# Decoder layer on one core: the transpose of the softmax reciprocals placed behind the second pair of scores of the next unit

## The chip, the cores and the metric

The kernel runs on one core of a Trainium2 chip. The time is the device time of one execution in microseconds (us). The kernel before took 1795.61 us, the median of 3 runs (1793.44 to 1797.07).

## What is computed

A decoder layer on x, 8 batches of 512 tokens with width 512, in float32: a dilated self-attention within segments of 128 tokens, a cross-attention over a context, and a feed-forward block whose activations and weights are quantised in blocks of 32. Each of the three is added to x. The edit touches the cross-attention alone (16 heads of 32, 512 queries, the first 512 rows of the context, causal):

```
qp = q @ Wq.T
kv = latent_kv @ Wkv_expand.T
k, v = jnp.split(kv, 2, axis=-1)
scores = jnp.einsum('bhqd,bhkd->bhqk', qh, kh) * inv_sqrt_d
scores = jnp.where(causal, scores, jnp.finfo(scores.dtype).min)
attn = jax.nn.softmax(scores, axis=-1)
out = jnp.einsum('bhqk,bhkd->bhqd', attn, vh)
return out.transpose(0, 2, 1, 3).reshape(b, sq, H) @ Wout.T
```

## The kernel before

First come the weights (0 to about 203 us). Then each batch has two stages: the cross-attention (about 93 us) and a stage with the feed-forward block of this batch and the self-attention and layer norms of the next (about 108 us). Every engine has a fixed program, written out by hand, and they wait for one another by semaphores.

**Units.** The cross-attention works on units (oc, qt): oc is a group of four heads (4 a batch), qt a tile of 128 queries (T = 4). By the causal mask a unit has (qt + 1) x 128 keys, so qt 0 is the smallest unit and qt 3 the largest. The work of three units overlaps. In the iteration of unit u:
- TensorE makes the scores of u + 1 in two pairs of heads (score2, L1099 to L1115), turns the reciprocals of u - 1 (turn_recip, L1132 to L1136) and multiplies the probabilities of u - 1 with v (values2, L1138 to L1155), and transposes the four heads' probabilities of u (turn_p2, L1117 to L1130). For the next oc it projects the queries (project_q, at qt 2, twelve matmuls of 512 columns) and the keys (project_k, at qt 0). In the last oc, qt 1 and 2, it makes part of the first output tile (output) in their place.
- VectorE finds the rows' maxima of the scores (maxima, L770), copies the transposed heads 0 and 2 into pt2 (take_probs, L783), and makes the reciprocals of the row sums and spreads them to 32 columns a head (recips, L789 and L792, tile recip_x). Once an oc it multiplies the values with the transposed reciprocals (take_out, L798, tile xn, which out_n shares).
- ScalarE makes the exponentials with their sums (exps, L969), copies the transposed heads 1 and 3 into pt2 (take_probs, L993) and the transposed reciprocals into recip_t (take_recip, L983), and casts keys and queries of the next oc (high_k, high_q).

**PSUM.** psum_plan (L57) lays down in which order the results take their turns in each piece of PSUM. A result may be written when the one ahead of it in that list has been read (until_free); who needs the reader's work waits by until_freed. A and B hold the first and second pair of scores (two banks each). C0 and C1 are one bank each: C0 takes heads 0 and 2 of the transposed probabilities, C1 takes heads 1 and 3 and, behind them, the transposed reciprocals. T and O, one bank each, take keys, queries and values (outT) of even and odd oc in turn: the keys of oc + 1 go into the bank from which take_out has read the values of oc - 1.

**Waits around the change.** turn_recip waits for its turn in C1 and for recip_x. values2 waits for the copies of heads 2 and 3 in pt2, and at qt 0 for its bank; it doesn't wait for the reciprocals. take_out waits for the last values product of its oc and for the copy of its last reciprocals in recip_t.

Of the kernel before, what the change touches and what calls it, by code (L numbers as in the profile page):

```python
# [56 lines left out]
def psum_plan(B, T, OC):  # L57

    plan = {s: [] for s in ("T", "O", "A", "B", "C0", "C1")}
    turn = [0]  # L60

    def self_attention(b, i):
        for label in self_attention_step(b, i, T):
            plan[("T", "C1")[turn[0] % 2]].append(label)
            turn[0] += 1

    P1_STEPS = 4 * T + 5
    for i in range(P1_STEPS):
        self_attention(0, i)

    def head(b, i):
        for t in HEAD_TILES[i]:
            plan[("C1", "A", "B", "C1")[t]].append(("xT2", b * T + t))

    for i in range(4 * T, P1_STEPS):
        head(0, i)
    for b in range(B):
        for oc in range(b * OC, (b + 1) * OC):

            plan["TO"[oc % 2]].append(("k", oc))  # L80
            plan["TO"[oc % 2]] += [("q", oc), ("outT", oc)]
            for qt in range(T):
                for pr in range(2):
                    plan["AB"[pr]].append(("scores2", oc, qt, pr))
                for hh in range(4):
                    plan[f"C{hh % 2}"].append(("probsT2", oc, qt, hh))
                plan["C1"].append(("recipT", oc, qt))
        for t in range(T):
            plan["TABO"[t]].append(("y", b * T + t))
        for i in range(P1_STEPS):  # L90
            if i < 4 * T:
                if i % 4 == 0:
                    plan["C0"].append(("xqT", b * T + i // 4))
                plan["AB"[i % 2]].append(("gateup", 4 * T * b + i))
            if INTER_LAG <= i < 4 * T + INTER_LAG:
                plan["C0"].append(("interT", 4 * T * b + i - INTER_LAG))
            if b + 1 < B:
                self_attention(b + 1, i)
                if i >= 4 * T:
                    head(b + 1, i)  # L100
        for t in range(T):
            plan["O"].append(("down", b * T + t))
    return plan


def decoder_layer(nc, x, ctx_t, wq_t, wkv_t, wo_t, w_gate, w_up, w_down, out):
# [3 lines left out]
    T = N // P  # L110
    C = D // P
    OC = C
# [13 lines left out]
    with es:  # L126
# [537 lines left out]
        with nc.Block() as block:  # L664
# [77 lines left out]
            def _(dve):  # L742
# [137 lines left out]
                for b in range(B):  # L880

                    first, end = b * UNITS, (b + 1) * UNITS
                    for pr in range(2):
                        maxima(first, pr)
                    for u in range(first, end):
                        oc, qt = units[u]
                        more = oc % OC + 1 < OC
                        if u + 1 < end:
                            maxima(u + 1, 0)
                        take_probs(u, 0)  # L890
                        if qt == 0 and oc % OC:
                            take_out(oc - 1)
                        if qt == 1 and more:
                            low_k(oc + 1)
                        if qt == 2 and more:
                            low_q(oc + 1)
                        if u + 1 < end:
                            maxima(u + 1, 1)
                        take_probs(u, 1)
                        recips(u)  # L900
                    take_out((b + 1) * OC - 1)

                    last = b + 1 == B
                    take_y(b * T)
                    moments3(b * T)
                    take_y(b * T + 1)
                    quantise_x(b * T)
                    take_y(b * T + 2)
                    moments3(b * T + 1)
                    round_x(b * T)  # L910
                    if not last:
                        attend_vector(dve, link, b + 1, 0)
                    take_y(b * T + 3)
                    if not last:
                        attend_vector(dve, link, b + 1, 1)
                    for i in range(P1_STEPS):
                        if i < CHUNKS:
                            gated(b * CHUNKS + i)
                        if 1 <= i <= CHUNKS:
                            round_inter(b * CHUNKS + i - 1)  # L920
                        if i in STATS_AT:
                            moments3(b * T + STATS_AT[i])
                        if i % 4 == 3 and i > 4:
                            take_down(b * T + i // 4 - 1)
                        if i >= 2 and not last:
                            attend_vector(dve, link, b + 1, i)
                            head(b + 1, i)
                        if i % 4 == 0 and i // 4 + 1 < T:
                            quantise_x(b * T + i // 4 + 1)
                        if i % 4 == 1 and i // 4 + 1 < T:  # L930
                            round_x(b * T + i // 4 + 1)

            @block.scalar
            def _(act):
# [94 lines left out]
                for b in range(B):  # L1029

                    first, end = b * UNITS, (b + 1) * UNITS
                    for pr in range(2):
                        exps(first, pr)
                    for u in range(first, end):
                        oc, qt = units[u]
                        if u > first:
                            take_recip(u - 1)
                        more = oc % OC + 1 < OC
                        if u + 1 < end:
                            exps(u + 1, 0)  # L1040
                        if qt == 1 and more:
                            high_k(oc + 1)
                        if qt == 2 and more:
                            high_q(oc + 1)
                        take_probs(u, 0)
                        take_probs(u, 1)
                        if u + 1 < end:
                            exps(u + 1, 1)
# [17 lines left out]
            def _(pe):  # L1066
# [160 lines left out]
                for b in range(B):  # L1227
# [4 lines left out]
                    for u in range(first, end):  # L1232
                        oc, qt = units[u]
                        more = oc % OC + 1 < OC
                        if u + 1 < end:
                            score2(u + 1, 0)
                        if u > first:
                            turn_recip(u - 1)
                            values2(u - 1)
                        if qt == 2 and more:  # L1240
                            project_q(oc + 1)
                        turn_p2(u, 0)
                        if u + 1 < end:
                            score2(u + 1, 1)
                        turn_p2(u, 1)
                        if qt == 0 and more:
                            project_k(oc + 1)
                        if not more and 0 < qt < 3:

                            output(b * T, [0, 1] if qt == 1 else [2])  # L1250
# [49 lines left out]
```

How the kernel before makes its waits and increments, by code:

```python
        def until_free(pe, label):  # L211
            s, k = slot_of[label]
            if k:
                pe.wait_ge(freed[s], k)
# [4 lines left out]
        def until_filled(eng, label):  # L219
            s, k = slot_of[label]
            eng.wait_ge(filled[s], k + 1)
# [1 line left out]
        def until_freed(eng, label):  # L223
            s, k = slot_of[label]
            eng.wait_ge(freed[s], k + 1)
# [60 lines left out]
            @block.sync  # L286
            def _(sp):
                for j in range(RAW):
                    load_weights(sp, j)
                sp.dma_start(wq_raw[:], wq_t.rearrange("(c p) n -> p c n", p=P)).then_inc(wq_loaded, 16)
                sp.dma_start(wkv_raw[:], wkv_t).then_inc(wkv_loaded, 16)
                sp.dma_start(wo_sb[:], wo_t.rearrange("(c p) n -> p c n", p=P)).then_inc(wo_loaded, 16)
                for j in range(STEPS - RAW):
                    sp.wait_ge(wy_ready, j + 1)
                    load_weights(sp, j + RAW)
                sp.wait_ge(wo_loaded, 16)
# [5 lines left out]
                def link(ins):  # L303
                    n[0] += 1
                    ins.then_inc(pool_chain, 1)
                    pool.wait_ge(pool_chain, n[0])
# [16 lines left out]
                def scaled_rows(j):  # L323
                    pool.wait_ge(wr_ready, j + 1)
                    if j >= 2:
                        pool.wait_ge(wclip_ready, j - 1)
                    pool.tensor_tensor(by_block(w_y[:, j % 2]), by_block(w_raw[:, j % RAW]), spread(w_r[:, j]),
                                       ALU.mult).then_inc(wy_ready, 1)
```

## Time and profile before

| | before |
|---|---|
| three runs, median (lowest to highest) | 1795.61 us (1793.44 to 1797.07) |
| the profiled execution | 1798.01 us |
| span of its trace | 1796.2 us |
| mean granted TensorE clock | 0.908 of full speed |
| TensorE matmuls (PE) | 1435.2 us, 80% of the span |
| TensorE weight loads (PEld) | 874.5 us, 49% |
| VectorE (DVE) | 1178.7 us, 66% |
| ScalarE (ACT) | 861.2 us, 48% |
| GpSimd (POOL) | 547.4 us, 30% |
| shares of the chain that ended last | PE 43%, DVE 29%, ACT 9%, issue 9%, POOL 2% |

The table is of one profiled execution; its span runs from the first to the last instruction of the trace, and 1.8 us lie around it. Busy shares are averages over stages with different limits. In the timelines, PE is a matmul or transpose and PEld the weight load ahead of it; consecutive instructions of one line stand in one row (x6: six of them), and a number in brackets is the time for which the engine had been idle before it, with what it waited for.

### The profile page before, as it was taken

To read this page: it belongs to the slowest core of one execution; us is meant where nothing else is said; L and a number is where in the kernel's file an instruction comes from. 1 tells how busy PE (TensorE), PEld (TensorE's weight loads), DVE (VectorE), ACT (ScalarE), POOL (GpSimd) and SP (SyncE) were. 2 spreads that over 40 slices of the span, in tenths; PEclk is the share of its full clock that TensorE was granted. 3 is DMA by queue.
4 is the path that set the end of the run, shared out by engine and by line. 5 is a ranking of instruction groups with operands and counts; after the bars stand their busy time and mean duration, and the time that the engine had idled before them with its cause. 6 is when DMAs were issued, how large, how long until landed. Compare 5 with 4: busy or idle time off the path is not lost.

```text
span 1796.2 us, 31869 instructions
## 1 busy us (share of the span) xinstructions
PE 1435.2 (80%) x11616; PEld 874.5 (49%) x11616; DVE 1178.7 (66%) x2539; ACT 861.2 (48%) x2098; POOL 547.4 (30%) x494
## 2 busy tenths in 40 slices
PE   1224899789988899889988899879988899789987
PEld 0113565446634565446644565446644565446633
DVE  8993455865578555865577556865578555865576
ACT  2442454455635554455635554455635554455522
POOL 5871000640046101640046101640046100640045
PEclk9999899998999899898998799897999899998998
DMA  5311000010000001010000000010000000000001
GB/s 181 112 46 36 1 1 25 7 25 1 2 24 13 18 1 24 7 24 1 2 24 13 18 2 24 7 24 1 2 24 13 18 1 25 7 19 1 2 1 24
DMA packets 25287, 36.10 MB, mean 20 GB/s; under 512 B 2480, under 2 KB 10672, under 8 KB 25136
## 3 DMA queue, kind: packets, MB, share of 16 engines
q1 hardware_dynamic: 25136, 34.09, 7.1%
q8 instruction: 95, 1.56, 0.4%
q14 instruction: 56, 0.46, 0.1%
HBM read 25.69 MB, written 8.39 MB: 19 GB/s over the span
## 4 chain that ended last, share of the span: by engine, by line
PE 43%; DVE 29%; ACT 9%; issue 9%; POOL 2%; DMA 0%; SPq 0%; ACTq 0%; DVEq 0%; POOLq 0%
PE psum L526 9%; PE psum L1110 7%; PE psum L1127 7%; PE psum L1148 5%; DVE top L820 5%; PE psum L1164 4%; DVE inter L846 3%; DVE nmx L770 3%; PE psum L1187 3%; PE psum L1209 2%; PE psum L1113 2%; DVE q L816 2%; ACT silu L1007 2%; DVE pt L783 2%; PE psum L1136 2%
## 5 line engine op out<-in xcount | busy, mean ns | idle before, releaser
L503 POOL TENSOR_TENSOR rstd<-var_eps,minus_half 128x1 f32<-128x1 f32 x96 | 59.8, 623 | 894.9 <-DVE var_eps L497 894.9
L969 ACT ACTIVATE p<-psum,nmx 128x384 f32<-128x384 f32 (+3 forms) x512 | 265.8, 526 | 68.4 <-DVE nmx L770 64.0
L770 DVE TENSOR_REDUCE nmx<-psum 128x2 f32<-128x256 f32 (+3 forms) x256 | 210.7, 823 | 114.6 <-PE psum L1113 114.6
L783 DVE COPY pt<-psum 128x128 f32<-128x128 f32 (+3 forms) x256 | 124.6, 487 | 193.9 <-PE psum L1127 193.5
L1127 PE MATMUL psum<-ident,p 128*128 128x128 f32 x1280 | 206.4, 289 | 21.1 <-ACT pt L993 18.1
L1110 PE MATMUL psum<-k_hl,q_hl 32*128 32x128 f32 (+3 forms) x1536 | 204.3, 373 | 16.4 <-DVE q_hl L757 11.7
L691 POOL TENSOR_TENSOR inter<-inter,rscale 128x512 f32<-128x512 f32 x128 | 141.3, 1104 | 209.8 <-DVE rscale L854 209.2
L1209 PE MATMUL psum<-wd_sb,iq_t 128*128 128x512 bf16 x512 | 147.6, 415 | 37.8 <-DVE x_res L863 28.1
L993 ACT COPY pt<-psum 128x128 f32<-128x128 f32 (+3 forms) x256 | 109.3, 427 | 141.6 <-PE psum L1127 140.2
L1127 PEld LDWEIGHTS psum<-ident,p 128*128 128x128 f32 x1280 | 143.8, 146 | 56.0 <-ACT pt L993 26.6
L1187 PE MATMUL psum<-wg_sb,xq_t 128*128 128x512 bf16 x512 | 148.9, 418 | 26.2 <-ACT xq_t L1000 21.7
L1110 PEld LDWEIGHTS psum<-k_hl,q_hl 32*128 32x128 f32 x1536 | 124.5, 199 | 77.2 <-issue 53.7
L1187 PE MATMUL psum<-wu_sb,xq_t 128*128 128x512 bf16 x512 | 147.6, 415 | 0.0
L846 DVE TENSOR_TENSOR inter<-psum,silu 128x512 f32<-128x512 f32 x128 | 86.6, 677 | 85.8 <-ACT silu L1007 85.2
L691 POOL TENSOR_TENSOR iq<-q,scale 128x512 bf16<-128x512 fp8e4 x128 | 142.8, 1115 | 0.4 <-DVE q L816 0.4
L1007 ACT ACTIVATE silu<-psum 128x512 f32<-128x512 f32 x128 | 76.0, 593 | 126.3 <-PE psum L1187 126.0
L1164 PE MATMUL psum<-wo_sb,xn 128*128 128x512 f32 x256 | 124.8, 639 | 6.5 <-DVE xn L798 6.5
L526 PE MATMUL psum<-x_t,wq_hl 128*128 128x512 f32 (+1 forms) x480 | 126.1, 421 | 1.4 <-DVE k_hl L764 1.1
L1015 ACT COPY iq_t<-psum 128x512 bf16<-128x512 bf16 x128 | 74.5, 582 | 87.3 <-PE psum L1198 87.3
L427 PE MATMUL psum<-ident_b,w_q 128*128 128x128 bf16 x192 | 26.3, 310 | 112.3 <-POOL w_q L334 108.3
L526 PEld LDWEIGHTS psum<-x_t,wq_hl 128*128 128x128 f32 x480 | 96.3, 232 | 29.0 <-issue 10.0
L1148 PE MATMUL psum<-pt,v_sb 128*32 128x128 f32 x2560 | 105.8, 296 | 0.0
(104 smaller groups left out, 2397.5 us busy)
## 6 DMA issues: line engine op xcount, KB each, us to landing
x_in<-in_x_dram SPq DMA_DIRECT2D x32, 256.0 KB, 4.1
out_dram<-x_res SPq DMA_DIRECT2D x64, 128.0 KB, 2.4
w_raw<-in_w_gate_dram SPq DMA_DIRECT2D x16, 256.0 KB, 2.8
w_raw<-in_w_up_dram SPq DMA_DIRECT2D x16, 256.0 KB, 3.2
w_raw<-in_w_down_dram SPq DMA_DIRECT2D x16, 256.0 KB, 3.8
ctx_in<-in_ctx_t_dram SPq DMA_DIRECT2D x8, 256.0 KB, 2.9
wq_raw<-in_wq_t_dram SPq DMA_DIRECT2D x1, 1024.0 KB, 8.0
wo_sb<-in_wo_t_dram SPq DMA_DIRECT2D x1, 1024.0 KB, 10.2
```

What stands on the lines that cost most here:

```text
L526: last = pe.matmul(dst, w, x, start=(n == 0), stop=(stop and n == len(terms) - 1))
L691: pool.tensor_tensor(dst.rearrange("p (n k) -> p n k", k=BLOCK), src.rearrange("p (n k) -> p n k", k=BLOCK), scales.unsqueeze(2).to_broadc ...
L770: dve.tensor_reduce(nmx2[:, u % UNITS, 2 * pr:2 * pr + 2], where(("scores2", oc, qt, pr))[:, :, 0:(qt + 1) * P], AX_X, ALU.max, negate=Tru ...
L783: free(dve.tensor_copy(pt2[:, hh, 0:m], where(label)[:, 0, 0:m]), label)
L846: free(dve.tensor_tensor(inter[:, r, :], where(label)[:, 1, :], silu[:, i % 2, :], ALU.mult), label)
L969: ins = act.activation(p2[:, (4 * u + hh) % P2_RING, 0:m], where(label)[:, hh % 2, 0:m], ACT.Exp, bias=nmx2[:, u % UNITS, hh:hh + 1], accu ...
L1110: pe.matmul(where(label)[:, j, 0:m], q_hl[rows, oc % 2, i, qt * P:(qt + 1) * P], k_hl[rows, oc % 2, k, 0:m], start=(n == 0), stop=False)
L1127: last = pe.transpose(where(label)[:, 0, kt * P:(kt + 1) * P], p2[:, (4 * u + hh) % P2_RING, kt * P:(kt + 1) * P], ident[:])
L1148: last = pe.matmul(where(("outT", oc))[rows, 0, qt * P:(qt + 1) * P], v_sb[:, kt, h * HD:(h + 1) * HD], pt2[:, hh, kt * P:(kt + 1) * P], s ...
L1164: last = pe.matmul(where(label)[:, 0, :], out_n[:, oc, t % T * P:(t % T + 1) * P], wo_sb[:, oc, :], start=(oc == 0), stop=(oc == OC - 1))
L1187: last = pe.matmul(where(label)[:, j, :], xq_t[:, t % 2, c * P:(c + 1) * P], w[:, c, m * CH:(m + 1) * CH], start=(c == 0), stop=(c == C - 1))
L1209: last = pe.matmul(where(label)[:, 0, :], iq_t[:, i % RING, j * P:(j + 1) * P], wd_sb[:, 4 * m + j, :], start=(m == 0 and j == 0), stop=(m ...
```

## The change

In TensorE's order turn_recip(u - 1) moves from its place ahead of values2(u - 1) to a place behind the second score2 of the iteration and ahead of the transposes of heads 2 and 3 of u. The turns in C1 follow: head 1 of u, the reciprocals of u - 1, head 3 of u. Only the very last reciprocals of a batch keep a turn behind head 3 of their own unit. On ScalarE take_recip(u - 1) moves from the start of the iteration to between the copies of heads 1 and 3. On VectorE take_out(oc - 1) moves behind the maxima of the second pair of scores, ahead of the copy of head 2. No instruction is added or taken away, and no wait changes its condition but for the turns in C1.

```diff
--- before.py
+++ after.py
@@ -83,8 +83,11 @@
                 for hh in range(4):
+                    if hh == 2 and (qt or oc % OC):
+                        plan["C1"].append(("recipT", *((oc, qt - 1) if qt else (oc - 1, T - 1))))
                     plan[f"C{hh % 2}"].append(("probsT2", oc, qt, hh))
-                plan["C1"].append(("recipT", oc, qt))
+                if qt == T - 1 and oc % OC == OC - 1:
+                    plan["C1"].append(("recipT", oc, qt))
@@ -888,14 +891,14 @@
                         take_probs(u, 0)
-                        if qt == 0 and oc % OC:
-                            take_out(oc - 1)
                         if qt == 1 and more:
                             low_k(oc + 1)
                         if qt == 2 and more:
                             low_q(oc + 1)
                         if u + 1 < end:
                             maxima(u + 1, 1)
+                        if qt == 0 and oc % OC:
+                            take_out(oc - 1)
                         take_probs(u, 1)
                         recips(u)
@@ -1033,8 +1036,6 @@
                         oc, qt = units[u]
-                        if u > first:
-                            take_recip(u - 1)
                         more = oc % OC + 1 < OC
@@ -1043,6 +1044,8 @@
                         take_probs(u, 0)
+                        if u > first:
+                            take_recip(u - 1)
                         take_probs(u, 1)
@@ -1235,13 +1238,14 @@
                         if u + 1 < end:
                             score2(u + 1, 0)
                         if u > first:
-                            turn_recip(u - 1)
                             values2(u - 1)
                         if qt == 2 and more:
                             project_q(oc + 1)
                         turn_p2(u, 0)
                         if u + 1 < end:
                             score2(u + 1, 1)
+                        if u > first:
+                            turn_recip(u - 1)
                         turn_p2(u, 1)
```

## Rows read from the trace of the kernel before

**Rows 1.** The page of the profile, its first line.
```profile
span 1796.2 us, 31869 instructions
```

**Rows 2.** Busy time by stage: us, busy by engine, granted clock, DMA share, GB/s.
```profile
404.00:497.00 93.00, 84.70 (x787) 57.21 (x787) 50.12 (x104) 54.06 (x179) 0.00 (x0) 0.89 0.01 1
...
699.00:807.00 108.00, 89.72 (x643) 48.35 (x644) 80.81 (x197) 47.89 (x78) 55.79 (x56) 0.91 0.10 23
...
900.00:1008.00 108.00, 91.03 (x625) 48.77 (x625) 80.00 (x196) 46.24 (x72) 55.88 (x56) 0.87 0.09 23
```

**Rows 3.** The waits, whole span: us in total, times, longest us.
```profile
PE psum L1136 <- DVE recip_x L792: 39.4, 64, 0.9
```

**Rows 4.** Timeline, qt 3: start us, us, engine, line, operation [idle, releaser].
```profile
447.60 0.55 DVE L783 COPY pt<-psum 128x384 f32<-128x384 f32 x1
...
448.63 0.30 PE L1136 MATMUL psum<-ident,recip_x 128*128 128x128 f32 x1 [0.86 <-DVE recip_x L792]
...
448.86 0.86 PE L1148 MATMUL psum<-pt,v_sb 128*32 128x128 f32 x24
```

**Rows 5.** Timeline: the same period, rest of qt 3, start of qt 0.
```profile
450.79 0.58 ACT L993 COPY pt<-psum 128x512 f32<-128x512 f32 x1 [0.76 <-PE psum L1127]
...
451.28 1.04 PE L1127 MATMUL psum<-ident,p 128*128 128x128 f32 x8
...
452.36 0.58 ACT L993 COPY pt<-psum 128x512 f32<-128x512 f32 x1 [0.99 <-PE psum L1127]
...
453.34 1.08 PE L1148 MATMUL psum<-pt,v_sb 128*32 128x128 f32 x32
```

**Rows 6.** Timeline: the same period, qt 0, up to the key projection.
```profile
454.92 0.68 DVE L798 TENSOR_TENSOR xn<-psum,recip_t 128x512 f32<-128x512 f32 x1
...
455.39 0.39 PE L1127 MATMUL psum<-ident,p 128*128 128x128 f32 x2
455.59 0.69 DVE L770 TENSOR_REDUCE nmx<-psum 128x2 f32<-128x512 f32 x1
...
455.66 0.96 PE L526 MATMUL psum<-ctx_hl,wkv_hl 128*128 128x512 f32 x3
```

**Rows 7.** Timeline: the same period, qt 1, up to the next values product.
```profile
457.70 0.27 ACT L983 COPY recip_t<-psum 128x128 f32<-128x128 f32 x1 [0.37 <-PE psum L1136]
...
460.62 0.44 PE L1127 MATMUL psum<-ident,p 128*128 128x128 f32 x2 [0.84 <-ACT pt L993]
...
460.99 0.96 PE L1110 MATMUL psum<-k_hl,q_hl 32*128 32x512 f32 x6
...
462.94 0.75 PE L1148 MATMUL psum<-pt,v_sb 128*32 128x128 f32 x16
```

**Rows 8.** Timeline: the last oc of the batch (qt 1, 2 and 3).
```profile
482.31 0.37 ACT L993 COPY pt<-psum 128x256 f32<-128x256 f32 x1
...
483.00 1.88 PE L1164 MATMUL psum<-wo_sb,xn 128*128 128x512 f32 x4
...
489.17 0.55 PE L1127 MATMUL psum<-ident,p 128*128 128x128 f32 x3 [0.21 <-ACT pt L993]
...
489.56 1.02 PE L1164 MATMUL psum<-wo_sb,xn 128*128 128x512 f32 x2
...
491.07 0.86 PE L1148 MATMUL psum<-pt,v_sb 128*32 128x128 f32 x24
...
492.99 0.58 ACT L993 COPY pt<-psum 128x512 f32<-128x512 f32 x1 [1.25 <-PE psum L1127]
...
495.18 0.30 PE L1136 MATMUL psum<-ident,recip_x 128*128 128x128 f32 x1 [0.78 <-DVE recip_x L792]
```

**Rows 9.** Chain that ended last, three query projections: start us, us, what.
```profile
642.03 4.01 PE psum L526 x12
...
843.45 4.01 PE psum L526 x12
...
1047.56 4.31 PE psum L526 x12
```

## The prediction

> **What bounds the kernel now.** I read the busy times by stage first, then the waits, then the timeline of one period. The profiled execution spans 1796.2 us [rows 1]. Each of the eight batches has an attention stage of about 93 us, in which TensorE's matmuls are busy 84.7 us [rows 2], and a longer second stage that the edit leaves alone. In the attention stage TensorE works through a fixed order, so its own row sets the end: whatever moves an instruction there moves all behind it. Where it idles, the waits say for whom; the largest single wait of this stage is the transpose of the reciprocals (turn_recip, L1136) waiting for VectorE's copy recip_x: 39.4 us in 64 places [rows 3]. The edit aims at that wait. So the question is what else those places wait for, and what the transpose meets where it is put instead. For that one period (four units, 440.6 to 463.6 us) is walked on TensorE's row, and the last one of the batch separately. A gap in another engine's row counts only if TensorE stands at its end.
>
> **Part 1, the old place.** In the iteration of qt 3 TensorE idles 0.86 us, transposes at 448.63 and starts the values product at 448.86 [rows 4]. Without the transpose the product still needs pt2 of head 2, which VectorE copies from 447.60 to 448.15. A copy's end is seen about 0.06 us later (the product with ctx starts at 455.66, after take_out's end at 455.60 [rows 6]). So it starts at 448.20: **-0.66 us**. In the iteration of qt 0 it needs ScalarE's copy of head 3, 452.36 to 452.94 [rows 5]; with 0.06 to 0.23 us of signalling, of which I take 0.15 for the later of two waits, it starts at 453.09, against 453.34: **-0.25**. I take no extra cost for going from the scores straight to the values product: the nearest row has 0.23 us between the transpose and the product [rows 4], so it lies between 0 and 0.2.
>
> **Part 2, the new place.** Now the order in bank C1 is head 1, reciprocals, head 3. Before, one use lay between two copies by ScalarE, and score2 and head 2 (bank C0) covered it; now there are two uses, with only head 2's transposes between the second pair. From the start of the reciprocals' transpose, its 0.30 us [rows 4], 0.04, ScalarE's copy of 0.27 [rows 7] and 0.06 make about 0.63 us until head 3's transposes may start. The transpose itself takes 0.11 us of TensorE's time (eight in 1.04 us, the last of them about 0.27 long [rows 5]), and head 2's take 0.11 for each of qt+1 tiles. Left uncovered: about 0.4, 0.3, 0.2 and 0.1 us for qt 0, 1, 2 and 3.
> - qt 3: head 1's copy ends at 451.37 and head 2's transposes start at 451.28 [rows 5]. The reciprocals, put ahead of them, wait 0.15 for that copy, take 0.11, and head 3 waits 0.08: **+0.35**.
> - qt 0 followed by a project_k (twice a batch, for oc 1 and 2): take_out now also stands behind the second maxima on VectorE. These start at 455.59 and keep it some 0.60 us; take_out is ready no sooner (455.39 + 0.58 for the copy of recip_t), runs 456.20 to 456.88, and project_k, which needs its bank, starts at 456.94 instead of 455.66 [rows 6]: **+1.28**. With no project_k behind it (oc 3): 0.63 instead of 0.11 from head 2's old start to head 3, **+0.52**. What is queued behind the moved take_out on VectorE (head 2's copy, the next reciprocals) ends before the next scores do.
> - qt 1: here TensorE already idles 0.84 us ahead of head 3 for ScalarE's copy of head 1, until 460.62 [rows 7], since that copy stands behind two exponentials, which wait for maxima, and behind high_k. So an earlier values product brings nothing: the reciprocals start at 460.62, drag head 2 behind them, and head 3 comes at 461.25: +0.63. The next scores start at 461.62 instead of 460.99 and last about 1.05 with the causal part; the values product follows at once, at 462.68, against 462.94 [rows 7]. Together **-0.25**.
> - qt 2: transpose 0.11 and head 3's wait of 0.2 are swallowed, since the next values product hangs on VectorE's copy behind the maxima of scores that came earlier: **0** (at most +0.3).
>
> **Part 3, the last oc.** No project_k there, so ScalarE's copy of head 1 hangs on the maxima in each iteration. qt 1: it ends at 482.68, the reciprocals start at 482.73, head 3 at 483.37, the output at 483.67 against 483.00 [rows 8]: +0.66. qt 2: head 3 waited for the same copy at 489.17 [rows 8]; all of that moves by 0.66, and the output comes another 0.63 later than head 3 did: 490.86 against 489.56. It lasts 0.9, and the values product follows it at 491.76 against 491.07: +0.69. qt 3: head 1's copy ends at 493.57 + 0.69, the reciprocals start at 494.31, head 3 at 494.95, its four transposes and its copy end 1.2 later, and the last reciprocals' transpose, which needs C1, starts at 496.23 against 495.18 [rows 8]. In all **+1.05**.
>
> **The sum.** Per batch: three passages from qt 3 to qt 0, 3 x (-0.66 + 0.35 - 0.25) = -1.68; the k waits, 2 x 1.28 + 0.52 = 3.08; three iterations of qt 1, 3 x (-0.25) = -0.75; the last oc +1.05. That is +1.70 us, times 8 = **+13.6 us** on the span of 1796.2. The table's profiled execution took 1798.0 with 1.8 outside its span, 2.4 over the median of the three runs, 1795.6; on that median the forecast is **1809 us**. Nothing is removed: the same 128 transposes and copies run. DMA queues and GpSimd have nothing in this stage that the edit passes. The open costs (0 to 0.2 us for going from scores to values, some 15 times a batch but mostly within a wait; up to 0.3 at qt 2; take_out's reach) give +1.1 to +2.4 per batch, so 1804 to 1815.
>
> **The rivals.**
> - **The clock falls further.** The granted clock of the attention stage is 0.89 of full speed, a mean over stretches at 2.4 and at 1.2 GHz. What a change in it costs shows once: the second stage at 900 to 1008 us was granted 0.87 against 0.91 one batch before [rows 2], and the query projections of that batch start 204.1 us apart instead of 201.4 [rows 9]: 2.7 us. The edit makes the longest stretch with few matmuls (after the scores of qt 0, to project_q) about 1.5 us longer. The same price in each batch: 13.6 + 21.6 = 35, so **1831**. Against it: the moved waits also close gaps elsewhere, and the mean hardly has to fall.
>  The Trainium skill states this rule in "TensorE: Matmul & The Clock Gate", section "A second HAM failure mode: psum-queue depth-cycling": cycling through PSUM banks with short idles between groups of matmuls makes the clock swing between full and half rate. The trace agrees so far that 0.89 is granted in a stage in which TensorE is nearly always busy; by the rule the change would come out at this rival's time.
> - **The clock rises**, by the same price with less dense work in front of it: 13.6 - 21.6, so **1788**.
> - **take_out is in time.** If project_k finds its bank as early as head 3 allows, 2 x (1.28 - 0.52) = 1.5 us a batch fall away and +0.2 is left: **1797**, no change. For it: VectorE idles a good deal here. Against it: maxima of 0.69 us stand right in front of take_out.
> - **The advances stay (the other side).** If the way through C1 is covered, by other work of TensorE between the reciprocals and head 3, only gains are left: 3 x (-0.91) for qt 3 and 0 and 3 x (-0.88) for qt 1, with 15 x 0.11 for the transposes: -3.7 a batch, **1766**. It decides at one point: whether TensorE comes to head 3 later than 0.63 us after the reciprocals. Against it: between them stand at most four transposes of 0.11, and at qt 1 ScalarE's copy of head 1 is late already.
>
> **How the numbers follow.** Forecast 0.60; take_out in time 0.12; clock falls 0.16, half of it not beyond 1823; clock rises 0.07; advances stay 0.05. The range leaves out the two faster cases and the far half of the falling clock, 0.20: 1797 to 1823. About 0.2% is what a measurement of this kernel can tell from no change, here 1792 to 1799. Faster 0.12, same 0.12, slower 0.76.
>
> **What would show it.** Right: the wait of the reciprocals' transpose for recip_x is gone, and in its place it waits for pt L993 about once a period for over 1 us and in the last oc three times; head 3's transposes wait for ScalarE's recip_t in most units; project_k waits for take_out (xn) by about 0.7 us twice a batch; the projections lie 0.4 to 0.5 us further apart. Wrong: head 3 never waits for recip_t, or the values product still starts at the old distance from the scores, or the stage is shorter at the same clock. A mean clock of the stage off 0.89 by more than 0.02 would spoil the size in either direction.

## The result and the profile after

The change takes 1824.34 us (median of 4 runs, 1823.63 to 1824.99) against 1794.53 us before (4 runs): a ratio of 1.0165, 95% interval 1.0147 to 1.0182. It is 30 us slower. The forecast had the sign and less than half of the size: 1809 us, with a range that ended at 1823. One of the four executions of one experiment (take_out back at its old place) took 2559 us and is left out of its figure.

The head of the page after; the columns are busy time, share of the span and number of instructions:

```profile
span 1822.0 us, 31800 instructions
## 1 busy us (share of the span) xinstructions
PE 1447.9 (79%) x11547; PEld 879.9 (48%) x11616; DVE 1180.2 (65%) x2539; ACT 862.9 (47%) x2098; POOL 547.3 (30%) x494
```

The attention stage of one batch before, from its first scores to its last values product (stretch, its length, busy time of each engine, granted clock, DMA share, GB/s), and of one batch after:

```profile
804.70:899.00 94.30, 85.94 (x799) 58.33 (x803) 50.55 (x105) 55.31 (x184) 0.00 (x0) 0.89 0.01 1
```

```profile
1023.80:1121.70 97.90, 89.50 (x803) 58.58 (x803) 50.72 (x105) 55.43 (x184) 0.00 (x0) 0.88 0.01 1
```

The stage is 3.6 us longer; six of the eight batches after have 97.8 to 97.9 us, where six before had 94.3 to 94.5. The other two after take 99.5 and 100.6 us at a granted clock of 0.86 and 0.85, the other two before 95.2 and 95.5 us at 0.87 (each to the end of its last instruction, which adds some 0.25). The eight attention stages together are 30.3 us longer. The stage behind them has 107 us in most batches of both kernels. VectorE and ScalarE are as busy as before. TensorE's matmuls are busy 3.6 us longer, though they are the same matmuls: in part they ran at a lower clock.

The waits after, in total, times and longest us:

```profile
ACT recip_t L986 <- PE psum L1139: 63.1, 128, 0.8
...
PE psum L1139 <- ACT pt L996: 40.9, 48, 1.2
PEld psum L1130 <- ACT recip_t L986: 36.8, 120, 0.5
```

The wait of the reciprocals' transpose for recip_x, 39.4 us before [rows 3], is gone. In its place the same transpose (now L1139) waits 40.9 us for ScalarE's copy of head 1, and the weight loads of head 3's transposes (PEld, L1130) wait for the copy of the reciprocals in 120 places; in 24 of these TensorE's matmuls stand still as well, 6.0 us in all.

The timeline after, one period of TensorE's work, of the same kind as in [rows 4 to 7], from one query projection to the next:

```profile
859.36 3.84 PE L529 MATMUL psum<-x_t,wq_hl 128*128 128x512 f32 x12
...
864.79 0.28 PE L1139 MATMUL psum<-ident,recip_x 128*128 128x128 f32 x1
...
866.74 0.86 PE L1151 MATMUL psum<-pt,v_sb 128*32 128x128 f32 x24
...
869.30 0.33 PE L1139 MATMUL psum<-ident,recip_x 128*128 128x128 f32 x1
...
870.57 0.62 PE L1113 MATMUL psum<-k_hl,q_hl 32*128 32x256 f32 x6
870.68 0.59 ACT L996 COPY pt<-psum 128x512 f32<-128x512 f32 x1 [0.74 <-PE psum L1130]
...
871.41 1.08 PE L1151 MATMUL psum<-pt,v_sb 128*32 128x128 f32 x32
...
873.46 0.28 PE L1139 MATMUL psum<-ident,recip_x 128*128 128x128 f32 x1
...
873.66 0.69 DVE L773 TENSOR_REDUCE nmx<-psum 128x2 f32<-128x512 f32 x1 [0.58 <-PE psum L1116]
...
874.10 0.33 PE L1130 MATMUL psum<-ident,p 128*128 128x128 f32 x1 [0.25 <-ACT recip_t L986]
874.27 0.68 DVE L801 TENSOR_TENSOR xn<-psum,recip_t 128x512 f32<-128x512 f32 x1
...
875.01 0.96 PE L529 MATMUL psum<-ctx_hl,wkv_hl 128*128 128x512 f32 x3 [0.58 <-DVE xn L801]
...
879.53 0.39 ACT L996 COPY pt<-psum 128x256 f32<-128x256 f32 x1
...
879.97 0.33 PE L1139 MATMUL psum<-ident,recip_x 128*128 128x128 f32 x1 [1.19 <-ACT pt L996]
...
881.03 1.18 PE L1113 MATMUL psum<-k_hl,q_hl 32*128 32x512 f32 x6
...
882.47 1.08 PE L1151 MATMUL psum<-pt,v_sb 128*32 128x128 f32 x16
...
883.48 1.88 PE L529 MATMUL psum<-x_t,wq_hl 128*128 128x512 f32 x4
```

The reader is to see three things. The values products start as soon as their copies are there (866.74, 871.41). The key projection stands until take_out is done (875.01). And at qt 1 TensorE idles 1.19 us until ScalarE's copy of head 1 ends; the reciprocals and head 2 start only then. The last rows tell something that the forecast did not have: the scores at 881.03 take 1.18 us where before they took 0.96, and sixteen values matmuls 1.08 where before they took 0.75 [rows 7]. The stretch from these scores to the next projection, before and after, with the granted clock third from the end:

```profile
460.99:463.62 2.63, 2.09 (x27) 1.11 (x26) 2.60 (x6) 1.77 (x6) 0.00 (x0) 0.95 0.01 3
```

```profile
881.03:883.48 2.45, 2.45 (x25) 1.21 (x24) 1.75 (x5) 1.51 (x5) 0.00 (x0) 0.62 0.01 3
```

Before, almost all of it ran at 2.4 GHz; after, some three quarters of it ran at 1.2 GHz.

The period is 24.1 us against 23.05. The chain that ended last has the projections of one batch after:

```profile
1040.05 3.91 PE psum L529 x12
1064.27 3.74 PE psum L529 x12
1088.44 3.63 PE psum L529 x12
```

### The profile page after: what moved, and what is told of

The parts are those of the page before. It is cut to its first block, busy times and chain, and to the rows that moved or that the text cites. A ratio compares the mean times of both kernels' runs of the same rounds, so it can differ in the third digit from the quotient of the medians.

```text
span 1822.0 us, 31800 instructions
## 1 busy us (share of the span) xinstructions
PE 1447.9 (79%) x11547; PEld 879.9 (48%) x11616; DVE 1180.2 (65%) x2539; ACT 862.9 (47%) x2098; POOL 547.3 (30%) x494
## 4 chain that ended last, share of the span: by engine, by line
PE 45%; DVE 25%; ACT 11%; issue 8%; POOL 2%; DMA 0%; ACTq 0%; SPq 0%; DVEq 0%; POOLq 0%
PE psum L529 9%; PE psum L1113 8%; PE psum L1130 7%; PE psum L1151 5%; DVE top L823 4%; DVE nmx L773 3%; PE psum L1167 3%; PE psum L1190 3%; DVE inter L849 3%; PE psum L1116 2%; PE psum L1212 2%; ACT p L972 2%; ACT silu L1010 2%; DVE xn L511 1%; PE psum L1139 1%
## 5 line engine op out<-in xcount | busy, mean ns | idle before, releaser
L1130 PE MATMUL psum<-ident,p 128*128 128x128 f32 x1280 | 224.5, 294 | 10.9 <-ACT recip_t L986 6.0
L1113 PE MATMUL psum<-k_hl,q_hl 32*128 32x128 f32 (+3 forms) x1536 | 211.8, 384 | 15.6 <-DVE q_hl L760 11.7
L1130 PEld LDWEIGHTS psum<-ident,p 128*128 128x128 f32 x1280 | 148.8, 146 | 63.6 <-ACT recip_t L986 36.8
L1190 PE MATMUL psum<-wg_sb,xq_t 128*128 128x512 bf16 x452 | 133.8, 417 | 40.6 <-ACT xq_t L1003 30.0
L1167 PE MATMUL psum<-wo_sb,xn 128*128 128x512 f32 x256 | 114.6, 596 | 6.5 <-DVE xn L801 6.5
L1212 PEld LDWEIGHTS psum<-wd_sb,iq_t 128*128 128x128 bf16 x512 | 51.9, 108 | 127.3 <-issue 54.3
```

The source lines that it names most:

```text
L1113: pe.matmul(where(label)[:, j, 0:m], q_hl[rows, oc % 2, i, qt * P:(qt + 1) * P], k_hl[rows, oc % 2, k, 0:m], start=(n == 0), stop=False)
L1130: last = pe.transpose(where(label)[:, 0, kt * P:(kt + 1) * P], p2[:, (4 * u + hh) % P2_RING, kt * P:(kt + 1) * P], ident[:])
L1167: last = pe.matmul(where(label)[:, 0, :], out_n[:, oc, t % T * P:(t % T + 1) * P], wo_sb[:, oc, :], start=(oc == 0), stop=(oc == OC - 1))
L1190: last = pe.matmul(where(label)[:, j, :], xq_t[:, t % 2, c * P:(c + 1) * P], w[:, c, m * CH:(m + 1) * CH], start=(c == 0), stop=(c == C - 1))
L1212: last = pe.matmul(where(label)[:, 0, :], iq_t[:, i % RING, j * P:(j + 1) * P], wd_sb[:, 4 * m + j, :], start=(m == 0 and j == 0), stop=(m ...
```

## The experiments

Two questions were open: how much of the 30 us is waits and how much clock, and which of the moves costs. The runs were made in four groups, each on one chip and beside runs of the kernel before: 1795.0 us for the first four kernels, 1797.2 for the next four, 1797.2 and 1795.8 for two each. Ratios are to the kernel before.

**The transpose directly behind the values product.** This takes the wait for recip_x away from the values product, and leaves C1, ScalarE and VectorE as before.

```diff
--- before.py
                         if u > first:
-                            turn_recip(u - 1)
                             values2(u - 1)
+                            turn_recip(u - 1)
```

> The kernel before with turn_recip directly behind values2 instead of ahead of it; turns in C1, ScalarE and VectorE as before. Theory (the loss of the change lies in where the transpose was put, not in taking it away from ahead of the values product): the values product no longer waits for recip_x and starts 0.66, 0.25 and 0.5 us earlier at qt 3, 0 and 1; the way through C1 (0.63 us) is covered by head 0's transposes alone, so head 1 waits 0.3 us at qt 0 and 0.15 us at qt 1. The projections come 22.7 us apart instead of 23.05, and the time is 1781 us (-1.7 us a batch). Rival (the values product wins nothing, as the maxima and exponentials set the pace): 1792 to 1796 us, projections 23.0 us apart.

Measured: **1765.3 us**, 0.9825 (0.9798 to 0.9853), 30 us faster than before. The theory holds in direction: the values product does win its time if the transpose goes to a place where the way through C1 is covered. Its size is double the forecast. The stage and two projections of this kernel:

```profile
791.70:882.80 91.10, 85.25 (x803) 56.72 (x803) 50.74 (x105) 55.59 (x184) 0.00 (x0) 0.91 0.01 2
```

```profile
829.20 3.00 PE L526 MATMUL psum<-x_t,wq_hl 128*128 128x512 f32 x12
...
832.04 0.82 PE L1127 MATMUL psum<-ident,p 128*128 128x128 f32 x6
...
850.78 4.13 PE L526 MATMUL psum<-x_t,wq_hl 128*128 128x512 f32 x12
```

The twelve matmuls of a projection take 3.65 us or more in every batch of the kernels before and after. Here the second projection of each batch takes 3.0, at 2.4 GHz throughout; the first still takes 3.6 to 4.3, and the third 3.0 in four batches and 4.1 in the other four. So a part of the gain is clock: the stage is granted 0.91, against 0.89. How much is waits can be read where this kernel and the kernel before with a filled wait (below) have the same clock. One stage of this kernel, then one of that:

```profile
989.54:1079.33 89.79, 83.94 (x803) 55.72 (x803) 50.73 (x105) 55.76 (x184) 0.00 (x0) 0.92 0.01 1
```

```profile
796.64:888.94 92.30, 86.44 (x819) 57.94 (x819) 50.75 (x105) 55.32 (x184) 0.00 (x0) 0.93 0.01 1
```

That is 2.5 us a batch, an estimate of 20 us in all for the waits, where 1.7 a batch was expected; about 10 us came by the clock.

**The transpose between head 2 and head 3.** The change, with less of TensorE's own work behind the transpose.

```diff
--- after.py
                     for hh in (2 * pr, 2 * pr + 1):
+                        if hh == 3 and u % UNITS:
+                            turn_recip(u - 1)
...
-                        if u > first:
-                            turn_recip(u - 1)
                         turn_p2(u, 1)
```

> The change, but with the transpose of the reciprocals between head 2 and head 3 instead of ahead of head 2; turns in C1 as in the change. Theory (the price is the way from the transpose through ScalarE's copy to head 3): nothing of TensorE's own work is left in between, so head 3 waits 0.54 us in every unit instead of 0.1 to 0.4, and the time is 12 us above the change: about 1837 us. Rival (the price is that head 2 is held back with the reciprocals at qt 1, and VectorE's copy behind it): head 2 goes out early again, and the time is 5 to 10 us below the change: 1815 to 1819 us.

Measured: **1845.0 us**, 1.0278 (1.0258 to 1.0298), 21 us slower than the change. So the price is the way through C1 to head 3: TensorE's matmuls now wait for the copy of the reciprocals in 120 places, 42.7 us. Head 2 goes out early again and nothing is won by it on balance; what it alone is worth isn't shown. The size is again larger than the waits that were worked out, and the clock of the stage fell to 0.87.

**Four wide matmuls in the wait of qt 1**, in the change and in the kernel before. They do no useful work; they fill time in which TensorE stands.

```diff
--- after.py
+                def fill(u, count):
+                    oc, qt = units[u]
+                    label = ("probsT2", oc, qt, 2)
+                    until_free(pe, label)
+                    for _ in range(count):
+                        pe.matmul(where(label)[:, 0, :], ident_b[:], wg_sb[:, 0, 0:512], start=True, stop=True)
...
+                        if qt == 1:
+                            fill(u, 4)
                         if u > first:
                             turn_recip(u - 1)
                         turn_p2(u, 1)
```

> The change with four more bf16 matmuls of 512 columns in each iteration of qt 1, into bank C0 (whose turn they take just ahead of head 2) and ahead of the transpose of the reciprocals: at 2.4 GHz they last 0.9 us and lie in the 1.2 us for which TensorE waits there anyway. Their results are overwritten. Theory (what the change lost beyond the forecast 13.6 us, some 16 us, is the lower granted clock, 0.878 in the attention stage against 0.891): the clock of the stage rises above 0.90, the projections come under 23.7 us apart instead of 24.15, and the time is 1805 to 1815 us. Rival (the excess is waits and switching between kinds of matmul): clock about as in the change or the time unmoved, 1822 to 1830 us.

> The kernel before with the same four matmuls at qt 1, ahead of head 2's transposes; TensorE waits 0.84 us there for ScalarE's copy of head 1. Clock theory: the stretches at 1.2 GHz ahead of and in the query projections vanish, the clock of the attention stage rises from 0.89 to above 0.92, and the time is 1780 to 1790 us. Rival (waits alone): 1794 to 1800 us at the same distance of the projections.

Measured: in the change **1789.2 us** (0.9971, 0.9957 to 0.9985), 35 us below the change without them; in the kernel before **1768.5 us** (0.9845, 0.9824 to 0.9866), 27 us faster than before. More work made both kernels faster. In the change the whole gain lies in the attention stages (32.9 us between the two traces); in the kernel before 16 of 28 us do, and 8 lie in the stages behind them and 4 ahead of the first batch. The stages, first in the change and then in the kernel before:

```profile
1005.30:1099.50 94.20, 88.48 (x819) 57.42 (x819) 50.82 (x105) 55.41 (x184) 0.00 (x0) 0.93 0.01 1
```

```profile
994.60:1086.60 92.00, 86.15 (x815) 57.91 (x819) 50.74 (x105) 55.21 (x184) 0.00 (x0) 0.93 0.01 2
```

Both are granted 0.93, and there the change costs 2.2 us a batch (94.2 against 92.0), where at their own clocks it costs 3.6. So about 2.2 us a batch, 18 us in all, are waits, and about 1.4 us, 11 us in all, came by the clock. The forecast for the waits was 1.7. The split is an estimate: it takes the added matmuls to cost both kernels the same. At qt 1 behind a key projection they cost neither anything: from the scores behind that projection to those behind the wait it stays 5.13 us in the change and 4.45 in the kernel before. In the first oc they run at 1.2 GHz and take twice as long, in both.

**The same four, narrow.** A control: about the same time (1.0 us for the four at 2.4 GHz, as for the wide ones), on a sixteenth of the array.

```diff
--- the change with the wait filled
-                        pe.matmul(where(label)[:, 0, :], ident_b[:], wg_sb[:, 0, 0:512], start=True, stop=True)
+                        pe.matmul(where(label)[0:HD, 0, :], ident_b[0:HD, 0:HD], wg_sb[0:HD, 0, 0:512], start=True, stop=True)
```

> The change with four matmuls at the same place and of the same 512 columns as in the run with the filled wait, but on 32 rows and 32 columns of the array instead of 128 by 128, so that they take the same time and fill the same wait with little work for the array. Clock theory (the gain of the filled wait came from the clock, which follows the work done in the array): the clock of the attention stage stays near 0.88 and the time within 4 us of the change, 1820 to 1828 us. Rival (it is enough that TensorE doesn't stand idle, or the four matmuls shift the order of the waits): about 1789 us as with the wide ones, the clock again near 0.93.

Measured: **1821.5 us**, 1.0141 (1.0108 to 1.0174).

```profile
813.70:911.20 97.50, 91.86 (x815) 58.77 (x819) 50.79 (x105) 55.23 (x184) 0.00 (x0) 0.89 0.00 1
```

The stage has 97.5 us and a clock of 0.89, close to the 97.9 and 0.88 without any. The order of the waits is the same in both filled kernels, so the 32 us between them come from what the four matmuls do in the array, by way of the clock. But the narrow ones weren't without effect. The start of a stage and the rest of it, first narrow, then wide:

```profile
813.72:835.20 21.48, 20.96 (x108) 12.53 (x109) 7.83 (x16) 9.65 (x35) 0.00 (x0) 0.52 0.00 1
835.20:911.50 76.30, 71.20 (x712) 46.30 (x711) 42.96 (x89) 45.72 (x149) 0.00 (x0) 1.00 0.01 1
```

```profile
803.55:818.40 14.85, 14.20 (x76) 8.44 (x76) 6.34 (x14) 6.71 (x26) 0.00 (x0) 0.54 0.00 0
818.40:898.10 79.70, 74.41 (x744) 48.86 (x743) 44.48 (x92) 48.76 (x158) 0.00 (x0) 1.00 0.01 2
```

In seven of the eight batches the narrow ones, too, left no stretch at 1.2 GHz behind the start of the stage, where every stage of the change has two; there the second period is 22.57 us in both. They lose at the start: the clock stays at 1.2 GHz until 21.5 us into the stage, with the wide ones until 14.8, and in the change until 18.3.

**take_out back at its old place, and take_out moved alone.** The two halves of one question: what does VectorE's part of the change cost?

```diff
--- after.py (first kernel); before.py with the signs exchanged (second kernel)
                         take_probs(u, 0)
+                        if qt == 0 and oc % OC:
+                            take_out(oc - 1)
...
                             maxima(u + 1, 1)
-                        if qt == 0 and oc % OC:
-                            take_out(oc - 1)
```

> The change with take_out back at its old place on VectorE, ahead of the maxima of the second pair. Theory (project_k waits because the last reciprocals of an oc are transposed and copied so late, not because of VectorE's order): take_out starts 0.15 us earlier and project_k still waits over 0.4 us; the time is within 4 us of the change. Rival (the maxima in front of take_out make the wait): project_k comes 0.8 us earlier twice a batch, -13 us, 1811 us.

> The kernel before with the move of take_out alone, behind the maxima of the second pair. Theory: these start at 455.6 in the period that was read and take_out only behind them, so project_k comes 1.2 us later, twice a batch, and little of it is made good, +2.5 to +3.0 us a batch: 1815 to 1820 us, and project_k waits for xn in 16 places. With a lower clock on top up to 1830. Rival (VectorE has room, the wait is swallowed by the ScalarE copy for which TensorE waits at qt 1): 1795 to 1800 us.

Measured: back at its old place **1825.0 us** (three executions, 1823.6 to 1834.4; ratio 1.0178, 1.0135 to 1.0221), which can't be told from the change; moved alone **1852.0 us** (1839.0 to 1864.2; 1.0305, 1.0234 to 1.0376). Within the change VectorE's order hardly matters: the key projection still waits for take_out in 16 places, 7.5 us in all against 9.3, since take_out has to wait for the late copy of recip_t anyway. Moved alone it costs 55 us, nearly twice the whole change. The stage of that kernel in one of its five worst batches (the others were granted 0.85 and 0.88), and its wait ahead of project_k:

```profile
1036.00:1140.70 104.70, 95.86 (x803) 64.20 (x803) 50.81 (x105) 55.48 (x184) 0.00 (x0) 0.79 0.00 1
```

```profile
PE psum L526 <- DVE xn L798: 18.5, 16, 1.2
```

The wait came as worked out, 1.2 us in 16 places, but the clock fell to 0.79, and most of the 10 us by which the stage is longer are slow matmuls.

**take_out moved alone, with the four wide matmuls.**

> The kernel before with the move of take_out alone (1852 us) and the four wide matmuls at qt 1. It tells waits from clock in that move, whose attention stage was granted only 0.79 to 0.85. Theory (the move costs 2.5 to 3 us of waits a batch, the rest of its 57 us is the clock): the clock of the stage comes back to above 0.91, and against the kernel before with the same four matmuls (1768 us) 20 to 26 us remain, 1788 to 1796 us. Rival (the waits are larger than was worked out): clock back as well, yet above 1805 us.

Measured: **1824.7 us**, 1.0156 (1.013 to 1.0183), 56 us above the kernel before with the same four. The rival's figure came, but not its reason. The stage has 97.7 us at a clock of 0.91 in most batches, against 92.0 at 0.93. The projections lie 23.2 us apart against 21.9, which is the 1.3 us of the key projection's wait. The rest, 3.7 us, stands behind the last projection. There take_out holds up VectorE's reciprocals, the reciprocals' transpose waits 0.85 us for recip_x instead of 0.26, and the clock is low just where the four matmuls are, so that they take twice as long and overrun their wait:

```profile
892.37 0.30 PE L1143 MATMUL psum<-ident,recip_x 128*128 128x128 f32 x1 [0.85 <-DVE recip_x L792]
...
895.90 1.49 PE L1122 MATMUL psum<-wg_sb,ident_b 128*128 128x512 bf16 x3 [0.22 <-issue]
```

One batch of the eight has the same wait of 0.86 us and no low clock behind it:

```profile
1021.08:1116.87 95.79, 86.18 (x815) 57.87 (x819) 50.76 (x105) 55.27 (x184) 0.00 (x0) 0.93 0.01 1
```

There the stretch behind the last projection is 32.75 us, against 32.15 in the kernel before with the same four and 35.9 in the other seven batches. So 0.6 of the 3.7 us are a wait and 3.1 are clock. The waits of this move are 2 x 1.3 + 0.6 = 3.2 us a batch, little above the 2.5 to 3 that were expected; what failed is that the clock would come back. The +1.28 of the key projection was right, and filled waits don't always restore the clock.

**ScalarE's copy of head 1 ahead of the cast of the keys**, in the change and in the winner.

```diff
--- after.py (and the same in the kernel with the transpose behind the values product)
-                        if qt == 1 and more:
-                            high_k(oc + 1)
                         if qt == 2 and more:
                             high_q(oc + 1)
                         take_probs(u, 0)
+                        if qt == 1 and more:
+                            high_k(oc + 1)
```

> The change with one exchange on ScalarE: at qt 1 it copies head 1 ahead of the cast of the next keys (high_k) instead of behind it. The transpose of the reciprocals waits up to 1.2 us for that copy there. Theory (the wait is real but the stage there is also held by VectorE's copy of head 2, which comes behind low_k and the maxima): the transpose waits 0.5 us less, the values product behind it waits that much more for VectorE, and the time is within 5 us of the change, 1819 to 1826 us. Rival (ScalarE's copy sets the pace at qt 1): 0.5 us are won three times a batch, 1812 us, and less at a higher clock.

> The transpose directly behind the values product (1765 us), with ScalarE's copy of head 1 ahead of the cast of the next keys at qt 1, an exchange that won 11 us in the change. TensorE still waits 0.50 us for that copy there. Theory (the copy sets the pace at qt 1): 0.3 to 0.5 us three times a batch, 1753 to 1758 us. Rival (VectorE's copy of head 2, which stands behind low_k, takes its place and holds the values product): 1763 to 1767 us.

Measured: in the change **1812.9 us** (1.0084, 1.0067 to 1.0101), 11 us less; the rival's figure. In the winner **1763.3 us** (0.9808, 0.978 to 0.9835), no difference to 1765; again the rival's. In the change the longest wait for that copy fell from 1.2 to 0.7 us, three times a batch, yet the stages take 96.4 to 97.9 us where most took 98.1 (each to the last instruction), less than the 1.5 us that the rival counted; 3.9 of the 10 us between the stages of the two traces are the two long batches, which don't come up here. How much of the 11 us is wait and how much clock isn't separated. In the winner only head 3 waits for the copy, 0.50 us, and the trace shows where that went: the values product (L1148) waits for VectorE's copy of head 2 instead, in the winner and then with the exchange:

```profile
PE psum L1148 <- DVE pt L783: 10.1, 24, 0.4
```

```profile
PE psum L1148 <- DVE pt L783: 24.0, 40, 0.9
```

**Both edits that won**, and then without the four matmuls in the first oc.

> Both edits that won: the kernel before with turn_recip directly behind values2, and the four wide matmuls in the wait of qt 1. The clock of the kernel with the transpose behind the values product is 0.906 in the attention stage. If the clock is what the four matmuls give, it rises to above 0.93 and the stage falls from 91.0 by 2 us: 1745 to 1755 us. Rival (the stage had lost its low stretches already, or its wait is now too short for 0.9 us of matmuls): 1760 to 1770 us.

> The transpose directly behind the values product and the four wide matmuls at qt 1, but not in the first oc of a batch. In the run with both edits the first query projection came 16.4 to 17.4 us after the first scores instead of 15.7, since the clock is low there anyhow and the four matmuls take twice as long and overrun their wait. If the clock theory holds, that loss goes and the rest stays: 1.0 to 1.7 us a batch below 1764, 1750 to 1757 us. Rival (the added matmuls shift the low stretches elsewhere in the stage): 1758 to 1766 us, at the same clock as without them.

Measured: **1764.4 us** (0.9824, 0.9797 to 0.9851) and **1763.1 us** (0.9814, 0.9799 to 0.9828). Both miss and go to the rivals: the two gains don't add. In these three kernels the stage is granted 0.91 in most batches, and 0.92 in two, three and none of the eight. With the four matmuls, no stretch at 1.2 GHz begins behind the first oc, and the second period is 21.15 us in every batch. But in the first oc they run at 1.2 GHz and cost time: the first projection comes 16.4 to 17.5 us after the first scores instead of 15.7 to 16.2. Without them in the first oc the clock there is low for 17 us in every batch, where the plain kernel has 13.7 in six of eight. So these matmuls bring nothing more, and the plain exchange of two lines is the version to keep: 1765 us, faster than the kernels before and after.

## Why the forecast had the sign and missed the size

The steps of one period, each with what it adds to the distance from the start of the query projection, from the rows of before at 440.56 to 463.62 us and of after at 859.36 to 883.48 us:

| step | forecast | measured |
|---|---|---|
| the query projection itself | 0 | -0.26 |
| values product at qt 3, no longer behind recip_x | -0.66 | -0.66 |
| reciprocals and head 3 through C1 at qt 3 | +0.35 | +0.43 |
| values product at qt 0 | -0.25 | -0.24 |
| key projection behind take_out | +1.28 | +1.28 |
| qt 1, up to its values product | -0.25 | +0.18 |
| from there to the next query projection | 0 | +0.33 |
| sum | +0.47 | +1.06 |

In the forecast's own terms, the step that failed is the price of the clock: the sum put it at nothing and priced all of TensorE's work at its durations in one period of the kernel before. The change spends 23.9 us of a stage at 1.2 GHz, the kernel before 20.5 (granted 0.878 and 0.892).

**Right.** The four terms in the middle, which rest on waits, came to within 0.1 us: both advances of the values product, the way through C1 at qt 3, and take_out's delay of the key projection down to its cause (maxima at 873.66, take_out at 874.27 behind them, the projection at 875.01). The waits named beforehand are the ones that are in the trace. The range given for going from scores straight to the values product, 0 to 0.2 us, held as well: 871.41 and 866.74 come no later than their copies allow.

**Wrong: the step from qt 1 to the projection.** It was put at -0.25 and then 0, on durations of the kernel before. Measured: +0.18 and +0.33. The wait itself came as forecast (key projection to reciprocals 4.96 us, as key projection to head 3 in [rows 6, 7]). But from the start of the scores to the values product it took 1.44 us (881.03 to 882.47) where 1.06 was put, and the sixteen values matmuls took 1.08 instead of 0.75 [rows 7]: 0.38 + 0.33 of a miss of 0.76. The stretch was granted 0.62 where the same work before was granted 0.95. The clock fell in front of these matmuls, where before it fell shortly before the projection; the time at 1.2 GHz behind the first oc is 6.8 us in both kernels, in six of the eight batches after, and it lies on other work. Twelve projection matmuls in turn got 0.26 us back. In the two kernels with filled waits, which are at 2.4 GHz here in all batches but one, a period is 22.57 us against 21.9: so about 0.67 of the longer period are waits (forecast 0.47), and some 0.4 are clock.

**Wrong: the first oc.** The forecast used the same -0.25 there. The first projection comes 16.2 us after the first scores, 15.6 before: +0.6. Two batches before were granted as little in this stretch as those after. A usual one before, one of these two, and one after, from the first scores to the first projection:

```profile
804.74:820.37 15.63, 14.51 (x98) 8.99 (x98) 7.73 (x16) 8.37 (x32) 0.00 (x0) 0.61 0.00 1
...
1210.16:1226.27 16.11, 15.83 (x97) 9.91 (x97) 7.73 (x16) 8.56 (x32) 0.00 (x0) 0.52 0.01 2
```

```profile
1023.75:1039.98 16.23, 15.58 (x96) 9.33 (x96) 7.42 (x16) 8.22 (x31) 0.00 (x0) 0.54 0.01 2
```

So about 0.5 of the 0.6 us are clock, and the advance of 0.25 isn't there at equal clock either: +0.1. Together, per batch: first oc +0.6 (forecast -0.25), two periods of +1.1 each (forecast +0.47), last oc with the passage to it +0.7 (forecast +1.0): 3.5 us against 1.7.

**The rival that was closest.** "The clock falls further" gave 1831 with 16% and its price from a single event of 2.7 us. It was the right mechanism at about half that price: +1.4 us a batch by the comparison at equal clock. The mean clock went from 0.89 to 0.88 only, within the 0.02 which the forecast allowed before it would call its size spoiled; that allowance was part of the error. A fall from 0.892 to 0.878 in the mean of a stage of 98 us is 1.4 us of TensorE's full speed, nearly as much as the whole forecast for the batch. Its 2.7 us were read from one batch of the kernel before and are no measure of what this edit does to the clock. The take_out rival (1797) is refuted by the 0.58 us ahead of project_k, and the advances (1766) didn't stay in the change, but stayed, once the transpose stood where its way through C1 was covered. That this kernel came to 1765, next to that rival's 1766, is in part luck: about a third of its gain is clock, and by waits alone it was expected at 1781.

The Trainium skill's page "TensorE: Matmul & The Clock Gate", section "A second HAM failure mode: psum-queue depth-cycling", blames such a loss on short idles between groups of matmuls. The trace agrees: TensorE never idles more than 1.2 us at a time in this stage and yet part of it is granted 1.2 GHz, and filling one of the waits, with wide or with narrow matmuls, took away the low stretches behind the start of the stage. What the pair adds is that the filling isn't all: the low clock at the start of the stage ended after 18.3 us without any, after 14.8 with the wide ones and only after 21.5 with the narrow ones.

Open is which single wait of the change brings the clock down; what was shown is that wide matmuls at one place of it, qt 1, bring back more than the change lost.

## What to carry to other kernels

When a step must pass through a shared buffer, its place in the order is as good as the work that stands between it and the buffer's next user; move it behind the work that it delayed, not past the next user's first half. Where small matmuls and waits alternate, price an edit twice: once in waits, once in the clock, since standing still can cost as much again, or more, in slow matmuls behind it, and don't call 0.01 of mean clock small. Before blaming waits, fill one with wide matmuls that do nothing: if the kernel gets faster, the clock was part of the bound.

## What was not expected of the hardware

Useless work made kernels faster. Four bf16 matmuls of 128x128 by 512 columns at qt 1 raised the clock of the attention stage from 0.88 or 0.89 to 0.93 and won 35 and 27 us; the same four on 32x32 of the array gave 0.89 in the change and won 3.

One move of a 0.68 us instruction on VectorE took the clock of the stage to 0.79 in five of eight batches and cost 55 us, while the wait of the key projection for it adds up to 18.5 us over the span.

A wait of TensorE has two prices in these rows. A copy's end is followed by the next transpose after 0.05 to 0.06 us where it ends the first of two waits (879.53 plus its duration of 0.39, then 879.97), and after 0.14 us where it ends the second: ScalarE's copy at 870.68 ends at 871.27 and the values product starts at 871.41.
